# Where the normalised rows and x are transposed inside a slot of the local attention stage

## Chip, cores and metric

The kernel runs on one core of one Trainium2 chip. The metric is the device time of one execution in microseconds (us). The engines are named as in the profile: PE is TensorE (matmul), PEld its weight load, DVE is VectorE, ACT is ScalarE, POOL is GpSimd, SP is SyncE, which here only issues DMAs.

## The reference, cut to what matters

```python
x = x + cross_attention(ctx_1024, layernorm(x), mask)   # 16 heads, 4096 keys
x = x + linear_attention(layernorm(x))                  # two kinds of keys and values
x = x + ffn_stack(layernorm(x))                         # the local stage: 6 layers

# the local stage, x of shape (4, 256, 256), 16 heads of 64, windows of 64
for i in range(6):
    x = attn_layer(shift_tokens(x), Wqkv[i], q_scale[i], k_scale[i], Wo[i]) + x
    x = ffn_layer(shift_tokens(x), ln_g[i], ln_b[i], W1[i], b1[i], W2[i], b2[i]) + x

def attn_layer(x, Wqkv, qs, ksc, Wo):
    q, k, v = split(x @ Wqkv, 3)                  # each (4, 16, 256, 64)
    q, k = rotary(l2norm(q) * qs), rotary(l2norm(k) * ksc)
    # a window of 64 queries looks at its own 64 keys and the 64 before them
    attn = softmax(where(mask, -big, 8 * q @ k.T))
    return (attn @ v) @ Wo

def ffn_layer(x, g, bln, W1, b1, W2, b2):
    a, gate = split((layernorm(x) * g + bln) @ W1 + b1, 2)   # 682 columns each
    return a * gelu(gate) @ W2 + b2
```

`shift_tokens` moves the upper half of the features down by one token.

## The kernel before

The kernel has a stage of cross attention and then one with the linear attention and the six local layers. The change lies in the local layers. One layer is four **slots**, one for each batch of 256 tokens (two tiles of 128). The order of work inside a slot is written out by hand, once for each engine, in a function `slot` of that engine's block; the engines meet only at semaphores, whose counts are given as `a` (the slot's own), `f` (of the slot before) and `n` (of the next). An engine works strictly in the order written.

A slot does three things at a time:

- the **attention** of its own batch: `turn_qk` transposes queries and keys, `scores(g)` makes the scores, DVE's `minima(pair)` (L2334) scales and masks them out of the scores' banks 2 to 5 and counts `s_read`, ACT's `exps(pair)` (L2053) takes the exponent, DVE's `inverse` and `share(pair)` (L2350) normalise, `turn_probs(pair)` (L1772) transposes into bank 6, ACT's `probs_out(pair)` (L2060) copies that to `pT`, `out(g)` (L1788) multiplies with the values, and `project_out` (L1799) with the output weights;
- the **projection** of the next batch: twelve units `project(n, nb, j)` (L1722) into banks 0 and 1 by turns (`DENSE + j % 2`), each copied by ACT's `qkv_out(j)` (L2032) or its like; then on DVE `twists`, `norms`, `cosines`, `sums` (L2300), `scaled_keys` (L2306) turn and scale queries and keys of each tile, with `rotate` on POOL (L2655), a power, between `norms` and `scaled_keys`;
- the **feed-forward** of the batch before: `moments` (L2377) and `normal` (L2393) on DVE, `turn_xn` (L1810) on TensorE, `xn_out` (L2077) on ACT, which makes the high part and the whole of the normalised rows, `xn_low` (L2399) on DVE, which makes the low part; then six pieces `widen(m)` (L1830) into banks 0 and 1, each followed by `gates(m)` (L2097, a Gelu) on ACT and `gated(m)` (L2407) on DVE; then `narrow` (L1841) and `add_ffn` (L2415).

Products are made of parts for precision. A projection unit is six matmuls of 512 columns, of high and low parts. A piece of `widen` takes, for each of its two halves, two matmuls high with high, two high with low, and then two with the low part of the rows; before the first of the latter, and only in `widen(0)`, TensorE waits for `xn_low`:

```python
for n, (px, pw) in enumerate(WIDE_PARTS):
    if m == 0 and px == LOW:
        pe.wait_ge(xnT_done, a + U)
```

`turn_x` (L1705) transposes x of the batch after the next, `x_out` on ACT (L2012, L2013) makes its high part and `x_low` on DVE (L2252, L2253) its low part, for the projections of the slot that follows.

`add_attention` (L2362) adds the attention to x. When it is done, SP sends the half of the features that is to be shifted by one token to the tile `late` (`shift`, L1627 and L1628), and the next slot's `moments` waits for that DMA.

Three kinds of slot have more: batch 0 makes the high parts of the widening weights on ACT (`widening_high`, L2090) and the low parts on POOL (`widening_low`, L2666); batch 2 splits the next layer's projection weights, whose DMAs are issued in the same slot, into high parts on ACT (`weights_high`, L2021) and low parts on DVE (`weights_low`, L2259); batch 3 makes the last of these low parts.

The part of TensorE's slot in question, before the change: unit 9, unit 10, `turn_probs(3)`, unit 11, `turn_xn` (bank 0), `out(1)`, `turn_probs(4)`, `turn_x` (bank 1), `turn_probs(5)`, `widen(0)`, `widen(1)`, `out(2)`, `turn_probs(6)`, `widen(2)`, `turn_probs(7)`, `widen(3)`, `out(3)`, `widen(4)`, `widen(5)`, `project_out`, `narrow`, and then `turn_qk` of the next slot. On ACT: `qkv_out(10)`, `probs_out(3)`, `qkv_out(11)`, `xn_out`, `probs_out(4)`, `x_out`, `exps(7)`, `probs_out(5)`, `gates(0)` (the Gelu needs its table loaded, since `exps` used another), `probs_out(6)`, `gates(1)`. On DVE: `sums`, `share(5)`, `xn_low`, `x_low`, `inverse(7)`, `o_out(1)`, `share(6)`, `gated(0)`.

## Time and profile before

| what | us |
|---|---|
| time, median of 3 runs | 2143.72 |
| lowest and highest | 2138.83 and 2144.59 |
| the profiled execution, its own time | 2145.24 |
| its span, first to last instruction | 2143.4 |
| TensorE busy | 2040.7 |
| VectorE busy | 1723.7 |
| ScalarE busy | 1392.7 |
| GpSimd busy | 550.3 |

The profile covers one execution. The 24 slots of the local stage begin at 781 us. A matmul's end is modelled in the profile, so the time from start to start of two of them is surer than a busy time. "Idle" is the time between the modelled end of an instruction and the start of the next on the same engine.

### The profile page before, as it was taken

The numbers are of one execution on the slowest core, as the hardware profiler recorded it, in microseconds if no ns is written. First come the engines' busy times: TensorE is split into PE (matmuls) and PEld (weight loads), VectorE is DVE, ScalarE is ACT, GpSimd is POOL, SyncE is SP. The second block draws the span as 40 slices with busy tenths as digits, with TensorE's granted clock in tenths as the row PEclk, the third lists the DMA queues.
The fourth block names the chain that finished last, engine by engine and source line by source line (L and its number), as shares of the span: only waits on it lengthen the run. The fifth ranks groups of instructions, "written<-read, shape, count | busy, mean of one in ns | idle before, by whom it ended". The sixth has DMA issues, their size and how long they took to land.

```text
span 2143.4 us, 51804 instructions
## 1 busy us (share of the span) xinstructions
PE 2040.7 (95%) x17400; PEld 1704.1 (80%) x17400; DVE 1723.7 (80%) x4874; ACT 1392.7 (65%) x4026; POOL 550.3 (26%) x317
## 2 busy tenths in 40 slices
PE   5999999999998998999999999999999999999988
PEld 4787887887886676888888888888888888888877
DVE  6786787787676498898889888898889888988883
ACT  3776567567564355676767676866777676767653
POOL 2111111111111334232323233232323242323220
PEclk9999999999999999999999999999999999999999
DMA  3000000000000410021102011201120111011010
GB/s 120 8 10 1 7 12 1 7 12 1 6 26 0 140 31 15 13 72 33 56 14 72 14 58 31 72 14 46 44 73 14 34 57 52 25 33 55 14 33 20
DMA packets 50017, 72.10 MB, mean 34 GB/s; under 512 B 9429, under 2 KB 36869, under 8 KB 49541
## 3 DMA queue, kind: packets, MB, share of 16 engines
q1 hardware_dynamic: 47429, 64.30, 9.9%
q10 hardware_dynamic: 2368, 4.98, 0.6%
q8 instruction: 124, 2.03, 0.4%
q14 instruction: 96, 0.79, 0.1%
HBM read 51.58 MB, written 2.10 MB: 25 GB/s over the span
## 4 chain that ended last, share of the span: by engine, by line
PE 47%; issue 7%; DVE 4%; DMA 3%; ACT 3%; POOL 2%; SPq 1%; DVEq 0%; ACTq 0%; POOLq 0%
PE ps_loc L1722 17%; PE ps_loc L1830 7%; PE ps_loc L1799 5%; PE ps_loc L1761 4%; PE ps_loc L1841 4%; PE ps_loc L1772 4%; DMA late<-y_all 3%; PE ps_loc L1741 3%; PE ps_loc L1788 3%; POOL rnorm L2655 2%; PE ps_loc L1342 1%; ACT xnT_high L2077 1%; ACT pT L2060 1%; ACT xnT_loc L2077 1%; DVE w_low L2259 0%
## 5 line engine op out<-in xcount | busy, mean ns | idle before, releaser
L2655 POOL TENSOR_TENSOR rnorm<-norm_floor,half_loc 128x32 f32<-128x32 f32 x48 | 300.5, 6261 | 582.7 <-DVE norm_floor L2270 385.2
L1722 PE MATMUL ps_loc<-w_high,xT 128*128 128x512 f32 x1152 | 379.3, 410 | 0.7 <-ACT qk L2032 0.6
L2053 ACT ACTIVATE prob_loc<-prob_loc,top_loc 128x128 f32<-128x128 f32 x768 | 299.2, 402 | 45.2 <-DVE top_loc L2334 43.2
L718 ACT ACTIVATE prob<-prob,new_top 128x256 f32<-128x256 f32 x512 | 252.2, 497 | 0.0
L1722 PEld LDWEIGHTS ps_loc<-w_high,xT 128*128 128x128 f32 x1152 | 203.9, 189 | 51.4 <-issue 9.3
L2334 DVE CUSTOM_DVE_ANT_0 prob_loc<-ps_loc,const,rnorm 128x128 f32<-128x128 f32 x768 | 218.8, 345 | 28.0 <-PE ps_loc L1761 25.8
L1722 PE MATMUL ps_loc<-w_low,xT 128*128 128x512 f32 x576 | 228.5, 397 | 0.0
L2045 ACT ACTIVATE qT_loc<-ps_loc 128x512 f32<-128x512 f32 x96 | 57.4, 598 | 238.1 <-PE ps_loc L1741 238.1
L923 DVE CUSTOM_DVE_ANT_0 prob<-ps_cross,bias 128x256 f32<-128x256 f32 x512 | 184.7, 420 | 20.7 <-PE ps_cross L494 11.1
L1799 PE MATMUL ps_loc<-wo,qT_loc 128*128 128x256 f32 x768 | 169.8, 379 | 1.3 <-ACT qT_loc L2067 1.3
L1179 POOL TENSOR_TENSOR o<-o,alpha 128x1024 f32<-128x1024 f32 x32 | 61.0, 1906 | 425.1 <-DVE o L962 333.4
L1799 PEld LDWEIGHTS ps_loc<-wo,qT_loc 128*128 128x128 f32 x768 | 144.1, 190 | 20.1 <-issue 1.4
L2053 ACT ACTIVATION_READ_ACCUMULATOR prob_loc<-prob_loc,top_loc 128x1 f32 x768 | 153.7, 200 | 0.0
L1772 PE MATMUL ps_loc<-const,prob_loc 128*128 128x128 f32 x768 | 123.5, 283 | 30.1 <-ACT pT L2060 21.0
L519 PE MATMUL ps_cross<-const,prob 128*128 128x128 f32 x1024 | 140.4, 280 | 2.8 <-issue 1.9
L2060 ACT ACTIVATE pT<-ps_loc 128x512 f32<-128x512 f32 x192 | 115.1, 600 | 40.3 <-PE ps_loc L1772 28.5
L2350 DVE TENSOR_TENSOR prob_loc<-prob_loc,total_loc 128x512 f32<-128x512 f32 x192 | 132.9, 692 | 3.1 <-DVE total_loc L2343 0.5
L519 PEld LDWEIGHTS ps_cross<-const,prob 128*128 128x128 f32 x1024 | 112.2, 142 | 25.6 <-issue 14.7
L1772 PEld LDWEIGHTS ps_loc<-const,prob_loc 128*128 128x128 f32 x768 | 85.1, 141 | 57.4 <-DVE prob_loc L2350 36.8
L1722 PEld LDWEIGHTS ps_loc<-w_low,xT 128*128 128x128 f32 x576 | 108.3, 188 | 25.7
L1841 PE MATMUL ps_loc<-w,kT_loc 128*128 128x256 f32 x552 | 123.1, 379 | 0.0
L534 PE MATMUL ps_cross<-probT,v 128*64 128x256 f32 x1024 | 121.1, 384 | 0.0
(214 smaller groups left out, 4869.0 us busy)
## 6 DMA issues: line engine op xcount, KB each, us to landing
w_raw<-in_ffn_Wqkv_dram SPq DMA_DIRECT2D x24, 512.0 KB, 5.7
w_raw<-in_ffn_Wqkv_dram SPq DMA_DIRECT2D x24, 256.0 KB, 3.9
wo<-in_ffn_Wo_dram SPq DMA_DIRECT2D x24, 256.0 KB, 3.5
v_mid<-v_even SPq DMA_DIRECT2D x24, 256.0 KB, 3.4
v_mid<-v_odd SPq DMA_DIRECT2D x24, 256.0 KB, 3.7
w<-in_ffn_W_dram SPq DMA_DIRECT2D x12, 341.0 KB, 3.3
w<-in_ffn_W_dram SPq DMA_DIRECT2D x6, 640.0 KB, 4.6
ctx_raw<-in_ctx_dram SPq DMA_DIRECT2D x12, 256.0 KB, 2.8
```

The costliest lines, as they stand in the source:

```text
L519: ins = pe.transpose(ps[:, TURN + t, (i * TT + lt) * P:(i * TT + lt + 1) * P], prob[:, lt, 2 * pair + i, t * P:(t + 1) * P], k.ident)
L718: ins = act.activation(prob[:, t, h, :], prob[:, t, h, :], ACT.Exp, bias=new_top[:, t, h:h + 1], scale=-1.0, accum_out=chunk_sum[:, t, h:h ...
L923: ins = dve.tensor_tensor_reduce(out=prob[:, t, h, :], in0=ps[:, banks[pair % 2] + i, t * CHUNK:(t + 1) * CHUNK], in1=key_bias, scale=1.0, ...
L1722: ins = pe.matmul(ps[:, DENSE + j % 2, :], xT[:, px, kk, t * P:(t + 1) * P], wqkv[pw][:, kk, col:col + 512], start=kk == 0 and n == 0, sto ...
L1772: ins = pe.transpose(ps[:, TURN, at:at + P], prob[:, 2 * (pair % RING) + i, t, :], k.ident)
L1799: ins = pe.matmul(ps[:, WIDE_OUT, t * D:(t + 1) * D], oT[:, pair, t * P:(t + 1) * P], wo[:, pair, :], start=pair == 0, stop=pair == PAIRS - 1)
L1830: ins = pe.matmul(ps[:, DENSE + m % 2, part * T:(part + 1) * T], w1_parts[pw][kk][:, col:col + P], xnT_parts[px][:, kk, :], start=n + kk == 0,
L1841: ins = pe.matmul(ps[:, FFN_OUT, t * D:(t + 1) * D], uT[:, m, t * P:(t + 1) * P], w2[:, m, :], start=m == 0, stop=m == FM - 1)
L2053: ins = act.activation(pr, pr, ACT.Exp, bias=top[:, h, t:t + 1], scale=-1.0, accum_out=total[:, h, t:t + 1])
L2060: act.activation(pT[:, pair % 2, :, :, :].rearrange("p i t q -> p (i t q)"), ps[:, TURN, :], ACT.Copy).then_inc(pT_done, 2)
L2334: ins = dve.tensor_tensor_reduce(out=prob[:, 2 * (pair % RING) + e, t, :], in0=ps[:, bank, cols], in1=band, scale=rnorm[:, b % 2, t, h:h + ...
L2655: pool.tensor_tensor(rnorm[:, b % 2, t, :], norm2_floor[:, :], half[:, :], ALU.pow).then_inc(rnorm_done, 8)
```

## The change

`turn_xn` moves between units 9 and 10 and writes bank 4 (`XN`), one of the scores' banks, which is free once `minima(5)` is done; `xn_out` on ACT moves in front of `qkv_out(11)` and reads that bank. `widen(0)` moves in front of `turn_probs(5)` and waits itself for the copies of the last projection units. `turn_x` moves behind `widen(5)` and writes bank 5 (`XT`); `x_out` moves to the end of ACT's slot and `x_low` on DVE in front of `add_attention`. `turn_qk`, which writes banks 4 and 5 first, waits before its second group for `x_low`. On DVE `xn_low` goes in front of `share(5)`, and `gated(4)` and `gated(5)` go in front of the `cosines` of the second tile. Outside the slots the old bank is kept.

```diff
+        XN, XT = 4, 5
...
-            def turn_x(a, b):
+            def turn_x(a, b, at=None):
 
                 pe.wait_ge(y_out, a + U)
-                pe.wait_ge(qkv_done, a)
+                if at is None:
+                    pe.wait_ge(qkv_done, a)
+                else:
+                    pe.wait_ge(s_read, at + 2 * 6)
+                bank = DENSE + 1 if at is None else XT
...
+                    if g == 1 and turned:
+                        pe.wait_ge(xT_done, a + 2 * U)
...
-            def turn_xn(a, ahead):
+            def turn_xn(a, bank=XN):
                 pe.wait_ge(xn_done, a + U)
-                if ahead:
-                    pe.wait_ge(qkv_done, a + 2 * U + SLOTS - 1)
-                pe.wait_ge(u_done, a)
+                if bank == XN:
+                    pe.wait_ge(s_read, a + U + 2 * 6)
+                else:
+                    pe.wait_ge(u_done, a)
...
                     pe.wait_ge(xnT_copied, a + U)
-                if m == 1 and turn:
-                    pe.wait_ge(xT_done, a + 4 * U)
+                    pe.wait_ge(qkv_done, a + 2 * U + SLOTS - 1 if ahead else a + U)
+                if m == 1 and ahead:
+                    pe.wait_ge(qkv_done, a + 3 * U)
...
                     project(n, nb, 9)
+                if ffn:
+                    turn_xn(f)
+                if ahead:
                     project(n, nb, 10)
                 turn_probs(a, 3)
                 if ahead:
                     project(n, nb, 11)
-                if ffn:
-                    turn_xn(f, ahead)
                 out(a, L, b, 1)
                 turn_probs(a, 4)
-                if turn:
-                    turn_x(L + U * (b + 2), (b + 2) % B)
+                if ffn:
+                    widen(f, fb, 0, ahead)
                 turn_probs(a, 5)
                 if ffn:
-                    widen(f, fb, 0, turn)
-                    widen(f, fb, 1, turn)
+                    widen(f, fb, 1, ahead)
...
-                    widen(f, fb, 4, turn)
-                    widen(f, fb, 5, turn)
+                    widen(f, fb, 4, ahead)
+                    widen(f, fb, 5, ahead)
+                if turn:
+                    turn_x(L + U * (b + 2), (b + 2) % B, a)
                 project_out(a, b)
...
                 probs_out(a, 3)
+                if ffn:
+                    xn_out(f, L if b else L - LAYER, fb)
                 if ahead:
                     qkv_out(n, nb, 11)
-                if ffn:
-                    xn_out(f, L if b else L - LAYER, fb)
                 if split:
                     weights_high(L + LAYER, 0)
                 probs_out(a, 4)
-                if turn:
-                    x_out(L + U * (b + 2))
                 exps(a, 7)
...
                     weights_high(L + LAYER, 11)
+                if turn:
+                    x_out(L + U * (b + 2), XT)
                 if b == 0:
                     widening_high(L, not ffn)
...
                     sums(n, 0)
-                share(a, 5)
                 if ffn:
                     xn_low(f)
+                share(a, 5)
                 if split:
                     weights_low(L + LAYER, 0)
-                if turn:
-                    x_low(L + U * (b + 2))
                 inverse(a, 7)
...
                     norms(n, 1)
-                    cosines(n, 1, 1)
-                    sums(n, 1)
-                    cosines(n, 1, 0)
                 if ffn:
                     gated(f, 4)
                     gated(f, 5)
                 if ahead:
+                    cosines(n, 1, 1)
+                    sums(n, 1)
+                    cosines(n, 1, 0)
                     q_sum(n, 1)
...
+                if turn:
+                    x_low(L + U * (b + 2), XT)
                 add_attention(a, b)
```

## Rows read from the trace of the kernel before

**Rows 1.** The page, busy us (share of the span) and instructions.
```profile
PE 2040.7 (95%) x17400; PEld 1704.1 (80%) x17400; DVE 1723.7 (80%) x4874; ACT 1392.7 (65%) x4026; POOL 550.3 (26%) x317
```

**Rows 2.** Waits of TensorE, 835 to 2069: total us, times, longest.
```profile
PE ps_loc L1772 <- ACT pT L2060: 17.9, 22, 1.7
...
PE ps_loc L1772 <- DVE prob_loc L2350: 2.9, 8, 0.7
PE ps_loc L1830 <- DVE kT_loc L2407: 1.3, 5, 0.3
```

**Rows 3.** Timeline of TensorE, layer 1, batch 1: start, length, count, idle before.
```profile
1087.37 0.60 PE L1772 MATMUL ps_loc<-const,prob_loc 128*128 128x128 f32 x4
1087.72 0.72 PE L1722 MATMUL ps_loc<-w_high,xT 128*128 128x512 f32 x2
...
1091.28 0.60 PE L1705 MATMUL ps_loc<-const,y_all 128*128 128x128 f32 x4
1092.51 0.63 PE L1772 MATMUL ps_loc<-const,prob_loc 128*128 128x128 f32 x4 [0.63 <-ACT pT L2060]
...
1096.96 0.66 PE L1772 MATMUL ps_loc<-const,prob_loc 128*128 128x128 f32 x4
1097.38 0.48 PE L1830 MATMUL ps_loc<-xnT_high,w_high 128*128 128x256 f32 x2
...
1097.93 0.40 PE L1830 MATMUL ps_loc<-xnT_low,w_high 128*128 128x256 f32 x2
...
1104.18 7.07 PE L1799 MATMUL ps_loc<-wo,qT_loc 128*128 128x256 f32 x32
```

**Rows 4.** Timeline of ACT in the same slot.
```profile
1089.95 1.02 ACT L2077 ACTIVATE xnT_high<-ps_loc,vec 128x256 fp32r<-128x256 f32 x2
...
1091.75 0.61 ACT L2060 ACTIVATE pT<-ps_loc 128x512 f32<-128x512 f32 x1
...
1094.30 0.63 ACT L2060 ACTIVATE pT<-ps_loc 128x512 f32<-128x512 f32 x1
1094.94 1.28 ACT L2097 ACT_TABLE_LOAD   x1
1096.23 0.47 ACT L2097 ACTIVATE gate<-ps_loc,vec 128x256 f32<-128x256 f32 x1
1097.74 0.60 ACT L2060 ACTIVATE pT<-ps_loc 128x512 f32<-128x512 f32 x1 [1.03 <-PE ps_loc L1772]
```

**Rows 5.** Timeline of DVE in the same slot.
```profile
1089.33 2.26 DVE L2300 TENSOR_TENSOR qk<-qk,work 128x2048 f32<-128x2048 f32 x1
1091.50 0.68 DVE L2350 TENSOR_TENSOR prob_loc<-prob_loc,total_loc 128x512 f32<-128x512 f32 x1
...
1092.95 0.42 DVE L2252 TENSOR_TENSOR xT<-ps_loc,xT 128x256 fp32r<-128x256 f32 x1 [0.16 <-ACT xT L2013]
...
1096.81 0.48 DVE L2407 SCALAR_TENSOR_TENSOR kT_loc<-ps_loc,vec,gate 128x256 f32<-128x256 f32 x1 [0.89 <-ACT gate L2097]
```

**Rows 6.** Timeline of DVE, layer 1, batch 3.
```profile
1202.40 2.26 DVE L2300 TENSOR_TENSOR qk<-qk,work 128x2048 f32<-128x2048 f32 x1
```

**Rows 7.** Timeline of TensorE, layer 1, batch 3, first matmuls of `project_out`.
```profile
1217.09 1.24 PE L1799 MATMUL ps_loc<-wo,qT_loc 128*128 128x256 f32 x5
```

**Rows 8.** Timeline of ACT, layer 1, batch 2.
```profile
1147.58 0.63 ACT L2021 ACTIVATE w_high<-w_raw 128x512 fp32r<-128x512 f32 x1 [0.40 <-DMA w_raw<-in_ffn_Wqkv_dram]
```

**Rows 9.** Timeline of DVE: layer 1, batch 1, then around the end of layer 2, batch 0.
```profile
1112.52 1.23 DVE L2306 TENSOR_TENSOR qk<-qk,rnorm 128x1024 f32<-128x1024 f32 x1 [1.00 <-issue]
...
1281.10 2.59 DVE L2306 TENSOR_TENSOR qk<-qk,rnorm 128x1024 f32<-128x1024 f32 x1 [1.00 <-issue]
1283.62 0.68 DVE L2362 TENSOR_TENSOR y_all<-ps_loc,y_all 128x512 f32<-128x512 f32 x1
...
1293.15 0.29 DVE L2377 BATCH_NORM_STATS2 stats_loc<-y_all 128x6 f32<-128x128 f32 x1
```

**Rows 10.** Timeline of POOL around the end of layer 2, batch 0.
```profile
1280.98 6.91 POOL L2666 TENSOR_TENSOR w_low<-w,w_high 128x682 fp32r<-128x682 f32 x4
```

More of the change, by code:

```diff
@@ L1724, in project, with turn_qk @@
                 ins.then_inc(qkv_full, 1 if j < SLOTS - 1 else U - SLOTS + 1)
-            def turn_qk(a, first):
+            def turn_qk(a, first, turned):
                 pe.wait_ge(rope_done, a + U)
@@ L1801, in project_out, with widen @@
                 ins.then_inc(y_full, U)
-            def turn_xn(a, ahead):
+            def turn_xn(a, bank=XN):
                 pe.wait_ge(xn_done, a + U)
-                if ahead:
-                    pe.wait_ge(qkv_done, a + 2 * U + SLOTS - 1)
-                pe.wait_ge(u_done, a)
+                if bank == XN:
+                    pe.wait_ge(s_read, a + U + 2 * 6)
+                else:
+                    pe.wait_ge(u_done, a)
                 for kk in range(KD):
                     for t in range(TT):
-                        ins = pe.transpose(ps[:, DENSE, kk * T + t * P:kk * T + (t + 1) * P],
+                        ins = pe.transpose(ps[:, bank, kk * T + t * P:kk * T + (t + 1) * P],
                                            xn[:, t, kk * P:(kk + 1) * P], k.ident)
                 ins.then_inc(xnT_full, U)
-            def widen(a, b, m, turn):
+            def widen(a, b, m, ahead):
                 if m == 0:
@@ L1874, in slot @@
                 n, nb = L + U * (b + 1), (b + 1) % B
-                turn_qk(a, b == 0 and not ffn)
+                turn_qk(a, b == 0 and not ffn, b < B - 1 or turn)
                 scores(a, 0)
@@ L1916, in slot @@
                 if ffn:
-                    widen(f, fb, 2, turn)
+                    widen(f, fb, 2, ahead)
                 turn_probs(a, 7)
                 if ffn:
-                    widen(f, fb, 3, turn)
+                    widen(f, fb, 3, ahead)
                 out(a, L, b, 3)
                 if ffn:
-                    widen(f, fb, 4, turn)
-                    widen(f, fb, 5, turn)
+                    widen(f, fb, 4, ahead)
+                    widen(f, fb, 5, ahead)
+                if turn:
+                    turn_x(L + U * (b + 2), (b + 2) % B, a)
                 project_out(a, b)
@@ L2001, in _ @@
             f = LAYERS * LAYER + U * (B - 1)
-            turn_xn(f, False)
+            turn_xn(f, DENSE)
             for m in range(FM):
@@ L2008, in _, with x_out @@
         def _(act):
-            def x_out(a):
+            def x_out(a, bank=DENSE + 1):
                 act.wait_ge(qkv_full, a)
                 act.wait_ge(xT_full, a + U)
-                act.activation(xT[:, HIGH, 0, :], ps[:, DENSE + 1, 0:T], ACT.Copy)
-                act.activation(xT[:, HIGH, 1, 1:T], ps[:, DENSE + 1, T:2 * T - 1], ACT.Copy).then_inc(xT_high, U)
+                act.activation(xT[:, HIGH, 0, :], ps[:, bank, 0:T], ACT.Copy)
+                act.activation(xT[:, HIGH, 1, 1:T], ps[:, bank, T:2 * T - 1], ACT.Copy).then_inc(xT_high, U)
             def weights_high(L, h):
@@ L2068, in o_out, with xn_out @@
                     .then_inc(o_done, 4)
-            def xn_out(a, L, b):
+            def xn_out(a, L, b, bank=XN):
                 if b == 0:
@@ L2076, in xn_out @@
                     for kk in range(KD):
-                        ins = act.activation(dst[:, kk, :], ps[:, DENSE, kk * T:(kk + 1) * T], ACT.Identity,
+                        ins = act.activation(dst[:, kk, :], ps[:, bank, kk * T:(kk + 1) * T], ACT.Identity,
                                              bias=vec[:, V_FB + kk:V_FB + kk + 1], scale=vec[:, V_FG + kk:V_FG + kk + 1])
@@ L2239, in _ @@
             f = LAYERS * LAYER + U * (B - 1)
-            xn_out(f, LAYERS * LAYER, B - 1)
+            xn_out(f, LAYERS * LAYER, B - 1, DENSE)
             for m in range(FM):
@@ L2248, in by_head, with x_low @@
                 return qk[:, t, :].rearrange("p (s h d) -> p s h d", s=2, d=DH)
[L2250 removed]
+            def x_low(a, bank=DENSE + 1):
                 dve.wait_ge(xT_high, a + U)
[L2252 to L2253 removed]
+                dve.tensor_tensor(xT[:, LOW, 0, :], ps[:, bank, 0:T], xT[:, HIGH, 0, :], ALU.subtract)
+                dve.tensor_tensor(xT[:, LOW, 1, 1:T], ps[:, bank, T:2 * T - 1], xT[:, HIGH, 1, 1:T], ALU.subtract)\
                     .then_inc(xT_done, U)
```

5 lines of the change are left out of this document (1 added, 4 removed).

## Prediction

> **What bounds the kernel now.** I read the page first: TensorE is busy for 95% of the span [rows 1]. So only what TensorE waits for, or does more or less of, can move the time. Next I asked for its waits in the 22 full slots of the local stage, from the second to the last but one [rows 2]. The largest entry is the transpose of probabilities behind ACT's copy to `pT`: 17.9 us in 22 waits, one a slot. The same transpose waits 2.9 us in 8 cases for DVE's shares, and `widen` waits 1.3 us in 5 cases for DVE's gated product. Everything else is under 5 us.
>
> Then I followed one slot, that of batch 1 in layer 1, on three engines in order of time. On TensorE [rows 3] `turn_x` (L1705) starts at 1091.28 and `turn_probs(5)` at 1092.51. Four transposes go 0.35 before the next unit can start (1087.37 to 1087.72), 0.44 before another transpose (an estimate), so the real standstill is 1.23 - 0.44 = 0.8 us; the 0.6 that the view calls idle begins only at the modelled end. On ACT [rows 4] the reason is seen: `xn_out` (L2077) holds the queue from 1089.95 to 1091.75, and only then comes `probs_out(4)`, which `turn_probs(5)` needs. `xn_out` itself was late, because `turn_xn` stood behind the last projection unit. On DVE [rows 5] `sums` (L2300) runs from 1089.33 for 2.26 us, then `share(5)`, `xn_low`, `x_low`. DVE is busy without a break in front of that point, so the end of `sums`, 1091.59, is a fixed date for all that follows it.
>
> **The change on TensorE.** No instruction is added or removed. `turn_xn` moves ahead of unit 10, `widen(0)` ahead of `turn_probs(5)`, `turn_x` from in front of `turn_probs(5)` to behind `widen(5)`. Work is the same but for neighbours (about 0.1 us a slot, dropped). Intended: 1.5 us of `widen(0)` covers the 0.8 us wait.
>
> What `widen(0)` now needs. Its normalised rows: `turn_probs(3)` runs some 0.36 us later than at 1087.37, its copy starts 0.78 behind (the distance 1096.96 to 1097.74 in [rows 3, 4]), takes 0.48, and `xn_out` takes 1.80 plus a tail of 0.13: 1090.9. TensorE comes to `widen(0)` at about 1091.1. In time. But its third pair of matmuls reads the low part, `xnT_low`: in the neighbour `widen(2)` that pair starts 0.55 behind the first (1097.38 to 1097.93), so here at 1091.65. `xn_low` now stands directly behind `sums`: it starts where `share(5)` started, 1091.50, takes 0.68 and ends at 1092.18. TensorE stands still for **0.5 us** inside `widen(0)`, a new wait in the old one's place. Queued behind it are `turn_probs(5)` and everything else of the slot. With 0.95 us of `widen(0)` left, `turn_probs(5)` starts at 1093.2 instead of 1092.51. `share(5)`, now second, ends at 1092.8 and is not late.
>
> **The next wait: the gate.** `widen(2)` waits for `gated(0)`. From `turn_probs(5)` to it there is a chain on ACT and DVE [rows 3 to 5]: copy starts after 0.78, table load after 0.64 more, 1.29 to the Gelu, 0.58 to DVE, 0.48 and 0.05 to TensorE: 3.82 us. TensorE's own work between the two, `widen(1)`, `out(2)` and `turn_probs(6)`, is 3.5 us. So `widen(2)` starts at 1093.18 + 3.82 = 1097.0; before it was 1097.38. That is 0.4 gained, and `turn_x`, paid earlier before, is paid now behind `widen(5)` with 0.42 (1096.96 to 1097.38 is such a turn). From `widen(2)` to `project_out` it is then 6.80 + 0.42 = 7.22: **1104.22 against 1104.18**. In short: `project_out` = end of `sums` + 5.41 + 7.22. Behind `project_out` TensorE runs to the end of the slot without a wait. A plain slot gains nothing: two waits of 0.5 and 0.35 replace one of 0.8.
>
> The table load is ACT's, 1.28 us, and the Gelu follows it at once, 0.01 us later [rows 4]. The Trainium skill, page "ScalarE: Activation LUTs", section "What ACT_TABLE_LOAD costs", counts a further drain of about 1.38 us for a change of set. By the page every `widen(2)` would come 1.4 us later and the kernel some 30 us; the trace disagrees, and the sum uses the trace.
>
> **By kind of slot.** *Batches 0 and 1* (10): +0.04 each, +0.4.
> *Batch 3* (5): `sums` ends at 1202.40 + 2.26 = 1204.66 [rows 6], so `project_out` at 1217.29 where it was 1217.09 [rows 7]: +0.2 each, +1.0.
> *Batch 2* (6): ACT also splits weights there, and `probs_out(4)` stands behind a split that waits for its DMA at 1147.58 [rows 8]. Before the change the chain to `gated(0)` is bound by ACT, and the departure of `x_out` (0.5 us) shortens it. Where the DMA sets the date (two slots) that is 0.5 - 0.42: -0.1 each; where it lands sooner (three) the split moves up too and I take -0.4; the last layer's, without split or `turn_x`, -0.35. Together -1.7.
> *First and last slot*: few or no projections, so TensorE starves and `widen(0)`, or the absence of `x_low`, fills part of a stall. Bounds 0 and 0.8 + 0.7; I take -0.7.
>
> **DVE's tail.** `x_low` goes from the middle to behind `scaled_keys(1)` and costs 0.68 there (an estimate: two instructions of 0.42 [rows 5], each of which overlaps its neighbour by 0.08). `scaled_keys(1)` waits for POOL's power, that for `norms(1)`, and those come 0.67 earlier, since `gated(1)` no longer waits as long: the two cancel, and `add_attention` keeps its date. `gated(4)` and `gated(5)` move behind `norms` and delay only work in front of `scaled_keys(1)`, which waits 1.00 us for POOL anyway [rows 9]. `narrow` did not wait for them, so no gain. `turn_qk`'s new wait for `x_low` is covered: `x_low` ends over 1 us ahead.
>
> `add_attention` matters, for it sends the shifted rows over DMA, and `moments` of the next slot waits for them: ended at 1284.30, used from 1293.15, 8.85 us later [rows 9]. That wait feeds the 2.9 us in [rows 2]. In batch 2 DVE has no slack at its end, so `add_attention` comes 0.2 us later against the slot's end and batch 3 pays: +1.0 in five slots. In batch 0 of the later layers there is a race: `scaled_keys(1)` took 2.59 us, not 1.23 [rows 9, 10], because POOL's `w_low` started at 1280.98, DVE at 1281.10, and both read SBUF. Now the power ends 0.67 earlier and the weights' split, set by `f_full`, 0.4 earlier at most: DVE at 1280.43, POOL at 1280.5 or later. If DVE is first, `add_attention` ends 1.4 us sooner and the waits of batch 1, about three quarters of the 2.9 us plus 0.16 hidden in each of four, go: -2.8. I take it, with 0.6.
>
> The Trainium skill, page "SBUF — State Buffer", section "Who interferes with whom", says that a DVE instruction with two SBUF inputs and a GpSimd one that reads SBUF exclude each other, and that the order of issue decides; by it the loser waits, as the 2.59 us show, and `x_low`, with one input in PSUM, is not touched.
>
> **Sum.** +0.4 + 1.0 - 1.7 - 0.7 + 1.0 - 2.8 = -2.8 us. Against the profiled execution (span 2143.4, time 2145.24) that is 2142.4. The median of the runs is 1.5 lower, 2143.72, which gives 2140.9; I say 2141.
>
> **Rivals.** *A, faster: the wait is really covered.* If `widen(0)` found its low rows in time, `turn_probs(5)` would start behind `share(5)`, 1.3 us earlier at most, and the gate chain would follow: 0.35 a slot, 22 slots, 8 us: 2133. If also the gate came in time, all of [rows 2]'s 17.9 + 1.3, with 0.17 hidden in each of 27, would go: 2143.7 - 24 = 2120. Against: `sums` stands ahead of `xn_low` on DVE in the new order too. Chance 0.2, nearly all for the first half.
> *B, slower: `x_low` at the end delays the shifted rows.* If DVE gains nothing before its tail, `add_attention` is 0.68 late everywhere. It decides where `moments` already waits, 8 slots plus one at the margin: 9 x 0.68 = 6.1, plus batch 3's 1.0: 2150.8. For: DVE's continuous tail in batch 2. Against: POOL's power sets the date in the others. Chance 0.1.
> *C, POOL wins the race.* Then -2.8 falls away: 2143.7, no change that could be told. It and my forecast share 0.7, forecast 0.42, C 0.28.
>
> **Range and chances.** Run to run 0.3% (6.4 us) is what can be told from no change: faster means below 2137.3, slower above 2150.1. Range 2133 (A's first half) to 2149 (most of B). Faster: A plus the low edge of the forecast, 0.25; slower: most of B, 0.08; same 0.67.
>
> **What would show it.** After: `turn_probs(5)` no longer waits for `pT`; instead `widen` waits about 0.3 us (idle; 0.5 real) a slot for `xnT_low`, and 0.1 or more for the gated product, in all slots. Slots of batches 0 and 1 keep their length where nothing else waits. `scaled_keys(1)` at 1.2 us in batch 0 shows the race won, and batch 1's wait for the shifted rows is gone. I am wrong if `widen(2)` starts without a wait (A), or if `moments` waits in most slots (B).

## The result, and the profile after

The kernel with the change takes 2148.54 us (median of 14 runs, 2145.31 to 2152.05); the kernel before, measured beside it, 2144.32 (14 runs, 2138.83 to 2147.91). The ratio is 1.0019, 95% interval 1.0010 to 1.0027: slower by 4.2 us. That is within the 0.3% which the prediction calls the same; but the interval leaves out 1, and a gain of 2.8 us was forecast.

The profiled execution has a span of 2143.9 us (2143.4 before) and a time of 2145.73 (2145.24). In it the part ahead of the local stage, whose code is unchanged, happened to be 2.0 us shorter (the stage begins at 779.1, not 781.1), so the stage itself has grown by 2.5 us, from 1362.3 to 1364.8. The comparison goes by its slots, from the first transpose of one `turn_qk` to that of the next, added up over the layers:

| slots | before | after | difference | forecast |
|---|---|---|---|---|
| batch 0, six | 331.1 | 331.2 | +0.1 | +0.2, less a part of the first slot's 0.7 |
| batch 1, six | 337.4 | 336.1 | -1.3 | +0.2 - 2.8 |
| batch 2, six | 337.8 | 334.9 | -2.9 | -1.7 |
| batch 3, five | 281.7 | 288.4 | **+6.7** | +2.0 |
| the last slot | 74.3 | 74.2 | -0.1 | the rest of the 0.7 |

Nearly everything that grew is in batch 3. The page first (the span, then busy us, share and instructions):

```profile
span 2143.9 us, 51810 instructions
PE 2049.4 (96%) x17400; PEld 1703.0 (79%) x17400; DVE 1720.5 (80%) x4874; ACT 1398.6 (65%) x4026; POOL 529.1 (25%) x317
```

Counts are those of [rows 1]. POOL is 21 us less busy with the same 317 instructions, which will matter below. Waits of TensorE after, 833 to 2070 (total us, times, longest):

```profile
PE ps_loc L1839 <- DVE xnT_low L2410: 7.6, 20, 0.6
PE ps_loc L1779 <- DVE prob_loc L2361: 5.0, 7, 0.9
PE ps_loc L1839 <- DVE kT_loc L2418: 3.4, 5, 1.0
```

Against [rows 2]: the 17.9 us behind `pT` are gone, and `widen` now waits for `xn_low` in nearly every slot, 0.32 idle as a rule (about 0.15 in batch 0 of four layers, 0.59 in batch 3). The entry for DVE's shares has risen from 2.9 to 5.0, and 0.9 is its longest.

**A plain slot went as forecast.** TensorE after, the slot of layer 1, batch 1, which answers to [rows 3]:

```profile
1090.80 0.40 PE L1839 MATMUL ps_loc<-xnT_high,w_low 128*128 128x256 f32 x2
1091.51 0.50 PE L1839 MATMUL ps_loc<-xnT_low,w_high 128*128 128x256 f32 x2 [0.32 <-DVE xnT_low L2410]
...
1092.56 0.60 PE L1779 MATMUL ps_loc<-const,prob_loc 128*128 128x128 f32 x4
...
1096.31 0.51 PE L1839 MATMUL ps_loc<-xnT_high,w_high 128*128 128x256 f32 x2
...
1103.51 0.38 PE L1806 MATMUL ps_loc<-wo,qT_loc 128*128 128x256 f32 x1
```

And DVE there, which answers to [rows 5]:

```profile
1088.59 2.26 DVE L2311 TENSOR_TENSOR qk<-qk,work 128x2048 f32<-128x2048 f32 x1
1090.77 0.68 DVE L2410 TENSOR_TENSOR xnT_low<-xnT_loc,xnT_high 128x512 fp32r<-128x512 f32 x1
1091.37 0.68 DVE L2361 TENSOR_TENSOR prob_loc<-prob_loc,total_loc 128x512 f32<-128x512 f32 x1
```

`sums` ends at 1090.85. By the prediction's formula `project_out` starts 5.41 + 7.22 later, at 1103.48; it starts at 1103.51. From `turn_probs(5)` to `widen(2)` it is 3.75 us (forecast 3.82). The slot is 55.41 long against 55.35. No idle time for the gated product shows in such a slot: the 3.4 us of that entry are the slots of batch 2 but the last, 0.6 to 1.0 each, where the kernel before has 0.26.

**Batch 3.** Layer 1, batch 3. The slot starts at 1173.05 before and at 1171.53 after. The first matmuls of its `turn_probs(0)`, before and then after:

```profile
1183.95 0.66 PE L1772 MATMUL ps_loc<-const,prob_loc 128*128 128x128 f32 x4 [0.15 <-DVE prob_loc L2350]
```

```profile
1183.70 0.66 PE L1779 MATMUL ps_loc<-const,prob_loc 128*128 128x128 f32 x4 [0.93 <-DVE prob_loc L2361]
```

That is 10.90 us into the slot before and 12.17 after: 1.27 of stall, and the slot grew by 1.16. What made the shares late is seen on DVE. Before, from the end of `norms` on (the last line is the first of `moments`):

```profile
1162.83 0.18 DVE L2270 TENSOR_SCALAR norm_floor<-norm 128x32 f32<-128x32 f32 x1
1162.93 1.23 DVE L2294 TENSOR_TENSOR qk<-qk,cos 128x1024 f32<-128x1024 f32 x1
...
1168.46 1.88 DVE L2259 TENSOR_TENSOR w_low<-w_raw,w_high 128x512 fp32r<-128x512 f32 x3
1170.27 1.21 DVE L2306 TENSOR_TENSOR qk<-qk,rnorm 128x1024 f32<-128x1024 f32 x1
1171.40 0.68 DVE L2259 TENSOR_TENSOR w_low<-w_raw,w_high 128x512 fp32r<-128x512 f32 x1
1172.01 0.68 DVE L2362 TENSOR_TENSOR y_all<-ps_loc,y_all 128x512 f32<-128x512 f32 x1
...
1181.40 0.29 DVE L2377 BATCH_NORM_STATS2 stats_loc<-y_all 128x6 f32<-128x128 f32 x1 [0.41 <-DMA late<-y_all]
```

After:

```profile
1160.86 0.18 DVE L2281 TENSOR_SCALAR norm_floor<-norm 128x32 f32<-128x32 f32 x1
1160.95 0.86 DVE L2418 SCALAR_TENSOR_TENSOR kT_loc<-ps_loc,vec,gate 128x256 f32<-128x256 f32 x2
1161.74 1.21 DVE L2305 TENSOR_TENSOR qk<-qk,cos 128x1024 f32<-128x1024 f32 x1
...
1166.66 2.39 DVE L2270 TENSOR_TENSOR w_low<-w_raw,w_high 128x512 fp32r<-128x512 f32 x3
1168.97 1.47 DVE L2317 TENSOR_TENSOR qk<-qk,rnorm 128x1024 f32<-128x1024 f32 x1
1170.36 0.80 DVE L2270 TENSOR_TENSOR w_low<-w_raw,w_high 128x512 fp32r<-128x512 f32 x1
1171.09 0.41 DVE L2263 TENSOR_TENSOR xT<-ps_loc,xT 128x256 fp32r<-128x256 f32 x1
...
1171.75 0.67 DVE L2373 TENSOR_TENSOR y_all<-ps_loc,y_all 128x512 f32<-128x512 f32 x1
...
1181.14 0.29 DVE L2388 BATCH_NORM_STATS2 stats_loc<-y_all 128x6 f32<-128x128 f32 x1 [1.17 <-DMA late<-y_all]
```

`add_attention` ends at 1172.69 before, 0.36 ahead of the slot's start, and at 1172.42 after, 0.89 behind it. The shifted rows are there 8.7 us later in both. The 1.25 us between the two are a sum. `norms` ends 1.30 earlier, counted from the start of batch 2's slot (-1.30). That slot is itself 0.85 shorter on TensorE, so batch 3 starts sooner (+0.85). `x_low` stands in the way (+0.66). Small gaps between dependent instructions come to +0.16. And the low parts and `scaled_keys(1)`, the same five instructions, now take 4.43 us from first start to the end of the group, not 3.55 (+0.88). This last term is nowhere in the prediction. POOL shows where it is from; before:

```profile
1163.15 6.30 POOL L2655 TENSOR_TENSOR rnorm<-norm_floor,half_loc 128x32 f32<-128x32 f32 x1 [19.00 <-issue]
1169.42 2.98 POOL L2643 TENSOR_TENSOR cos<-const,head_scale 128x128 f32<-128x128 f32 x1
```

After:

```profile
1161.18 5.43 POOL L2666 TENSOR_TENSOR rnorm<-norm_floor,half_loc 128x32 f32<-128x32 f32 x1 [17.66 <-issue]
1166.57 0.48 POOL L2654 TENSOR_TENSOR cos<-const,head_scale 128x128 f32<-128x128 f32 x1
1167.02 1.49 POOL L2657 TENSOR_TENSOR sin<-const,head_scale 128x64 f32<-128x64 f32 x2
...
1169.32 2.02 POOL L2657 TENSOR_TENSOR sin<-const,head_scale 128x64 f32<-128x64 f32 x2
```

Before, POOL's power starts at 1163.15, while DVE's first `cosines` is running, which reads two SBUF operands (1162.93 to 1164.16), and it takes 6.30 us. POOL's first table (L2643) then takes 2.98 us beside DVE's low parts, and most of the tables come after `add_attention`'s start. After, the power starts at 1161.18, while `gated(4)` is running, which reads PSUM, and takes 5.43. In both kernels the rest of it runs beside `cosines` and `sums`. What goes with the 0.87 us is therefore the instruction that runs when the power starts. It is so in all eleven traces: the 48 powers of each take 6.28 to 6.30 us where a `twists` or a `cosines` of 1.22 us with two SBUF operands began 0.2 us before them, and 5.42 to 5.43 where it was an instruction that reads PSUM.

After, POOL comes to the tables at 1166.57, just as DVE starts its low parts at 1166.66, and this time it is DVE that loses: three parts 2.39 instead of 1.88, `scaled_keys` 1.47 instead of 1.21, a fourth part 0.80 instead of 0.68. That a power which starts beside a two-operand instruction takes longer fits what the Trainium skill says on the page "SBUF — State Buffer", section "Who interferes with whom" (the second port pair of DVE is GpSimd's only one, and one excludes the other). By that section whoever issues first has the pair for its whole instruction, and here the rows differ: the `cosines` that starts 0.56 us into the power takes 1.21 us, no more than elsewhere. That the loser pays only a part of the other's time, 0.88 us beside 4.8 us of tables, is in the rows alone.

**Batch 1.** The race at the end of batch 0, in layer 2, on DVE and then on POOL, which answers to [rows 9, 10]:

```profile
1279.49 1.23 DVE L2317 TENSOR_TENSOR qk<-qk,rnorm 128x1024 f32<-128x1024 f32 x1
...
1281.30 0.68 DVE L2373 TENSOR_TENSOR y_all<-ps_loc,y_all 128x512 f32<-128x512 f32 x1
```

```profile
1280.36 6.16 POOL L2677 TENSOR_TENSOR w_low<-w,w_high 128x682 fp32r<-128x682 f32 x4 [0.96 <-ACT w_high L2101]
```

DVE starts 0.87 us ahead of POOL, not 0.12 behind it, and the 2.59 are 1.23 again. Counted from the slot's start, the power begins at 44.82 (45.19 before) and `scaled_keys(1)` at 50.33 (51.58). `add_attention` ends 2.64 ahead of batch 1's slot instead of 0.61. `moments` of batch 1 no longer waits in layers 2 to 4; in the last layer the race is still lost, with POOL 0.07 us ahead (`scaled_keys(1)` 2.65).

### The profile page after: what moved, and what is told of

It reads as the page before. It is cut to its first block and busy times, and to the rows that moved or that the text cites. A ratio compares the mean times of both kernels' runs of the same rounds, so it can differ in the third digit from the quotient of the medians.

```text
span 2143.9 us, 51810 instructions
## 1 busy us (share of the span) xinstructions
PE 2049.4 (96%) x17400; PEld 1703.0 (79%) x17400; DVE 1720.5 (80%) x4874; ACT 1398.6 (65%) x4026; POOL 529.1 (25%) x317
## 3 DMA queue, kind: packets, MB, share of 16 engines
HBM read 51.58 MB, written 2.10 MB: 25 GB/s over the span
## 5 line engine op out<-in xcount | busy, mean ns | idle before, releaser
L2666 POOL TENSOR_TENSOR rnorm<-norm_floor,half_loc 128x32 f32<-128x32 f32 x48 | 281.3, 5860 | 572.4 <-DVE norm_floor L2281 381.7
L923 DVE CUSTOM_DVE_ANT_0 prob<-ps_cross,bias 128x256 f32<-128x256 f32 x512 | 184.7, 420 | 20.1 <-PE ps_cross L494 10.6
L1839 PE MATMUL ps_loc<-xnT_high,w_high 128*128 128x256 f32 x528 | 116.5, 302 | 7.1 <-DVE kT_loc L2418 3.4
```

The lines of the kernel that those rows point to most:

```text
L923: ins = dve.tensor_tensor_reduce(out=prob[:, t, h, :], in0=ps[:, banks[pair % 2] + i, t * CHUNK:(t + 1) * CHUNK], in1=key_bias, scale=1.0, ...
L1839: ins = pe.matmul(ps[:, DENSE + m % 2, part * T:(part + 1) * T], w1_parts[pw][kk][:, col:col + P], xnT_parts[px][:, kk, :], start=n + kk == 0,
L2666: pool.tensor_tensor(rnorm[:, b % 2, t, :], norm2_floor[:, :], half[:, :], ALU.pow).then_inc(rnorm_done, 8)
```

## The experiments

Three names stand in the quoted expectations. D: the loss comes from DVE's end, a late `add_attention` and with it late shifted rows in batch 3. W: it comes from TensorE's own new waits in `widen` and from paying `turn_x` behind `widen(5)`. L: what makes DVE's end late is in the main the move of `gated(4)` and `gated(5)`, by way of POOL's earlier tables and DVE's low parts.

Two parts of the profile vary between executions by more than the edits in them explain: the lead-in (778.7 to 783.5 us), whose code is the same in all, and the last slot (73.3 to 77.8). So beside each median stands the length of the 23 slots between. It is 1288.1 us before and 1290.6 after, +2.6.

**The change in three parts.** Each part is made alone on the kernel before. The rows' part: `turn_xn`, `widen(0)`, `xn_out` and `xn_low` moved as in the change; x is turned where it was, into bank 5:

```diff
                 if ffn:
+                    turn_xn(f)
+                if ahead:
                     project(n, nb, 10)
...
                 turn_probs(a, 4)
                 if turn:
-                    turn_x(L + U * (b + 2), (b + 2) % B)
+                    turn_x(L + U * (b + 2), (b + 2) % B, a)
+                if ffn:
+                    widen(f, fb, 0, ahead)
                 turn_probs(a, 5)
```

> Only the rows' part of the change: turn_xn, xn_out, xn_low and widen(0) as in the changed kernel; turn_x, x_out and x_low at their old places (in bank 5); gated(4) and gated(5) behind the cosines again. Theory D (the loss comes from DVE's tail in batch 2, where x_low and the work on POOL make add_attention late, so that moments of batch 3 waits for the shifted rows): the slots of batch 3 stay near 56.4 us as in the kernel before (57.6 in the changed one), the wait of moments there stays at 0.4 us, POOL's power stays at 6.3 us, and the time is that of the kernel before within 3 us, rather below it. Rival W (the new waits inside widen(0) and before widen(2) are the loss): the loss of 2 to 6 us stays.

Measured: 2135.96 us (4 runs), ratio to before 0.9957 (0.9940 to 0.9974); 23 slots 1280.0. Waits of TensorE, 835 to 2061:

```profile
PE ps_loc L1839 <- DVE kT_loc L2418: 5.1, 15, 0.7
...
PE ps_loc L1779 <- DVE prob_loc L2361: 2.2, 7, 0.7
...
PE ps_loc L1839 <- DVE xnT_low L2410: 0.8, 4, 0.3
```

This part is 8.8 us faster. `turn_x` stands between `turn_probs(4)` and `widen(0)` here: the 0.4 us that it takes are covered, because the same time would else be a wait for `xn_low`, which has fallen from 7.6 us to 0.8. The loss did not stay, as W had it. D's marks are there (the power takes 6.3 us, `moments` of batch 3 waits 0.34 to 0.49, its slots take 55.8 to 56.0), but the size was missed: it expected the time of the kernel before within 3 us. Against this part alone the changed kernel's 23 slots are 10.6 us longer: 8.6 of it in batch 3, 2.0 in batches 0 and 1, nothing in batch 2.

The x part: `turn_x` behind `widen(5)`, `x_out` and `x_low` at the ends of their queues, the rest as before:

```diff
-                if turn:
-                    turn_x(L + U * (b + 2), (b + 2) % B)
                 turn_probs(a, 5)
...
                     widen(f, fb, 5, ahead)
+                if turn:
+                    turn_x(L + U * (b + 2), (b + 2) % B, a)
...
+                if turn:
+                    x_low(L + U * (b + 2), XT)
                 add_attention(a, b)
```

> Only the x part: turn_x behind widen(5), x_out at the end of ACT's slot, x_low in front of add_attention; the rows and the gated products as before. turn_probs(5) is released by the same copy at the same time, so turn_x's 0.42 us, hidden in that wait before, is paid in full: 0.4 a slot, 23 slots, 9.7 us. Theory D adds that add_attention comes 0.68 later in every slot and moments waits more where it waited before: 0.6 to 0.7 us in some nine slots, 6 us, so 13 to 16 us slower than before. Rival W: about 10 us slower with the slots of batch 3 longer by 0.4 only.

Measured: 2155.68 us (4 runs), ratio 1.0051 (1.0034 to 1.0068); 23 slots 1296.2. Waits of TensorE, 835 to 2080:

```profile
PE ps_loc L1779 <- ACT pT L2067: 26.1, 22, 1.6
PE ps_loc L1779 <- DVE prob_loc L2357: 6.7, 10, 1.8
```

It is 10.9 us slower. The wait for `pT` is 26.1 us where [rows 2] have 17.9: taking `turn_x` away from in front of it only makes it longer, by 0.37 a slot, and `turn_x` is paid in full elsewhere. Slots of batch 0 grow by 0.4 each. `moments` of batch 3 waits 0.63 to 0.68 instead of 0.34 to 0.52. The time is W's (about 10), not D's 13 to 16: in layer 1 `add_attention` ends 56.4 us into batch 2's slot in both kernels, with `x_low` now in front of it, and against the slot's end it comes 0.2 to 0.3 us later, not 0.7. The slots of batch 3 grow by 0.5 on average.

The third part, `gated(4)` and `gated(5)` alone in front of the `cosines` of tile 1:

```diff
                     norms(n, 1)
-                    cosines(n, 1, 1)
-                    sums(n, 1)
-                    cosines(n, 1, 0)
                 if ffn:
                     gated(f, 4)
                     gated(f, 5)
                 if ahead:
+                    cosines(n, 1, 1)
+                    sums(n, 1)
+                    cosines(n, 1, 0)
```

> The kernel before with one edit on DVE: gated(4) and gated(5) directly behind norms of the second tile, ahead of the cosines. Theory L (POOL's power and a DVE instruction with two inputs in SBUF exclude each other): the power of the second tile takes 5.4 us instead of 6.3, because the instruction beside its start now reads PSUM; scaled_keys is 0.9 us earlier in batches 0, 1 and 3 and the wait of moments in batch 1 goes (2 to 3 us gained); in batch 2 POOL's tables start earlier and run against DVE's low parts and scaled_keys, which lose some 0.9 us, so batch 3 is longer by 0.5 to 0.9 us each (2.5 to 4.5 lost). Net 0 to 2 us slower. Rival: the power's length has nothing to do with its neighbour, it stays at 6.3 and no slot changes by more than 0.1.

Measured: 2148.67 us (10 runs), ratio 1.0016 (1.0006 to 1.0026); 23 slots 1290.1. DVE and then POOL at the end of batch 2, layer 1:

```profile
1170.63 2.39 DVE L2259 TENSOR_TENSOR w_low<-w_raw,w_high 128x512 fp32r<-128x512 f32 x3
1172.94 1.47 DVE L2306 TENSOR_TENSOR qk<-qk,rnorm 128x1024 f32<-128x1024 f32 x1
```

```profile
1165.15 5.43 POOL L2655 TENSOR_TENSOR rnorm<-norm_floor,half_loc 128x32 f32<-128x32 f32 x1 [18.49 <-issue]
```

With no other edit the power is 5.43, the parts 2.39 and `scaled_keys` 1.47, digit for digit as with the whole change. Batch 1 is 2.2 us shorter, batch 2 1.0, and batch 3's five slots are 5.3 longer (1.1 each; at most 0.9 was expected).

In the 23 slots the three parts measure -8.0, +8.1 and +2.0, together +2.1, where the change measures +2.6: they add up within 0.5. The medians add up less closely, to +6.0 against +4.2, with four runs for each of the first two. The change holds a half that wins 0.4% and a half that loses it again.

**The new wait in `widen(0)`.** On the kernel after, DVE's `sums` go behind `share(5)` and `xn_low`:

```diff
-                if ahead:
-                    sums(n, 0)
+                share(a, 5)
                 if ffn:
                     xn_low(f)
-                share(a, 5)
+                if ahead:
+                    sums(n, 0)
```

> The changed kernel with another order on DVE: share(5), xn_low, sums of the first tile, instead of sums, xn_low, share(5). By the chain of the prediction (project_out is the end of sums plus 5.4 plus 7.2) the low rows are then set by ACT's copies, which end 30.0 us into the slot, so xn_low ends at 30.8 instead of 31.26; the wait inside widen(0) (0.33 idle) is gone, turn_probs(5) and widen(2) come 0.3 to 0.4 earlier, in batch 3 0.6. 22 slots: 7 to 9 us faster than the changed kernel, 3 to 6 faster than before. Rival: sums, 2.26 us, now delays inverse(7) and share(6), turn_probs(6) or the gated product waits instead, and nothing or less than 2 us is gained.

Measured: 2140.09 us (10 runs), ratio to before 0.9978 (0.9969 to 0.9988), 8.5 us under the changed kernel; 23 slots 1282.6. DVE and TensorE, layer 1, batch 1:

```profile
1090.37 0.69 DVE L2410 TENSOR_TENSOR xnT_low<-xnT_loc,xnT_high 128x512 fp32r<-128x512 f32 x1 [0.92 <-ACT xnT_loc L2088]
1090.98 2.29 DVE L2311 TENSOR_TENSOR qk<-qk,work 128x2048 f32<-128x2048 f32 x1
```

```profile
1090.85 0.39 PE L1839 MATMUL ps_loc<-xnT_high,w_low 128*128 128x256 f32 x2
1091.12 0.50 PE L1839 MATMUL ps_loc<-xnT_low,w_high 128*128 128x256 f32 x2
```

As expected (7 to 9 us under the changed kernel). The wait for `xn_low` is gone from the list of waits, and a plain slot falls from 55.41 to 54.99. So `sums` was the fixed date that the prediction took it for. `moments` of batch 3 still waits 1.2 us: the two losses are separate.

**The late rows, undone two ways.** On the kernel after, first `gated(4)` and `gated(5)` at their old place in batch 2 only:

```diff
-                if ffn:
+                if ffn and not split:
                     gated(f, 4)
                     gated(f, 5)
                 if ahead:
                     cosines(n, 1, 1)
                     sums(n, 1)
                     cosines(n, 1, 0)
+                if ffn and split:
+                    gated(f, 4)
+                    gated(f, 5)
+                if ahead:
```

> The changed kernel, with gated(4) and gated(5) behind the cosines again in the slots of batch 2 alone. Theory L: there POOL's power takes 6.3 us again, its tables start 0.9 us later and lose against DVE's low parts instead of winning; scaled_keys of that slot takes 1.2 instead of 1.47, add_attention ends 0.7 to 0.9 us earlier, and the slots of batch 3 fall from 57.6 to 56.8 us. The other slots stay. 4 us faster than the changed kernel, that is the kernel before within 2 us. Rival (x_low alone makes batch 3 late): batch 3 stays above 57.4.

Measured: 2143.31 us (10 runs), ratio to before 0.9999 (0.9988 to 1.0009), 5.2 us under the changed kernel; 23 slots 1285.2. POOL, then DVE, at the end of batch 2, layer 1:

```profile
1160.11 6.30 POOL L2670 TENSOR_TENSOR rnorm<-norm_floor,half_loc 128x32 f32<-128x32 f32 x1 [17.65 <-issue]
1166.38 2.98 POOL L2658 TENSOR_TENSOR cos<-const,head_scale 128x128 f32<-128x128 f32 x1
```

```profile
1165.42 1.88 DVE L2270 TENSOR_TENSOR w_low<-w_raw,w_high 128x512 fp32r<-128x512 f32 x3
1167.23 1.21 DVE L2317 TENSOR_TENSOR qk<-qk,rnorm 128x1024 f32<-128x1024 f32 x1
...
1179.02 0.29 DVE L2388 BATCH_NORM_STATS2 stats_loc<-y_all 128x6 f32<-128x128 f32 x1 [0.61 <-DMA late<-y_all]
```

Everything goes back to the numbers of before: 6.30 and 2.98 on POOL, 1.88 and 1.21 on DVE. The wait of `moments` falls from 1.2 to 0.6, and a slot of batch 3 from 57.6 to 56.6. The other slots keep their lengths within 0.15, except batch 1 of the last layer, 0.3 shorter, where DVE won the race this time. `add_attention` ends 0.16 ahead of the slot: 1.05 of the 1.25 us are undone by this edit alone, and the rival of this experiment, `x_low` as the only cause, is out. The 0.20 that are left are the figure of the prediction.

Then, on the kernel after, `x_low` behind `add_attention`:

```diff
+                add_attention(a, b)
                 if turn:
                     x_low(L + U * (b + 2), XT)
-                add_attention(a, b)
```

> The changed kernel with x_low behind add_attention instead of in front of it. Theory D: add_attention of batch 2 ends 0.7 us earlier, moments of batch 3 waits 0.5 instead of 1.2 us, and the slots of batch 3 fall from 57.6 to 57.0, 3 us in all; the price is in turn_qk of batch 3, whose second group now waits for x_low, up to 0.5 us a slot there. Between 1 and 3.5 us faster than the changed kernel. Rival: the copies of keys, not add_attention, set batch 3, and it does not fall.

Measured: 2144.12 us (10 runs), ratio to before 0.9999 (0.9987 to 1.0010), 4.4 us under the changed kernel; 23 slots 1287.5. The wait of `moments` is 0.51 to 0.56, `add_attention` ends 0.23 behind the slot's start (0.66 less), and slots of batch 3 are 0.6 shorter. The price in `turn_qk` came too: it waits 2.3 us in 6 cases for `x_low`. So rival B's price for `x_low` is real, 0.66 us. In the plain slots `add_attention` also ends 0.66 earlier without it (3.24 ahead of the slot, not 2.58), but nothing waits for it there.

**Better versions.** Three kernels were built on the rows' part. The first also has `gated(4)` and `gated(5)` early except in batch 2, and the seventh low part of the weights at the start of batch 3 instead of in front of batch 2's `add_attention`:

```diff
                 if late:
+                    weights_low(L + LAYER, 6)
                     weights_low(L + LAYER, 7)
...
-                if split:
-                    weights_low(L + LAYER, 6)
                 add_attention(a, b)
```

> The rows' part alone, with gated(4) and gated(5) ahead of the cosines in all slots but those of batch 2, and the low part of piece 6 moved from the end of batch 2 to the start of batch 3. Theories D and L: no slot waits for the shifted rows any more (0.3 to 0.8 us before in nine slots), batch 1 takes 55.2 and batch 3 55.7 us; 3 to 4 us faster than the rows' part alone, 11 to 13 faster than before. Rival: moments was no more than a cover for something else (minima, share), and the time is that of the rows' part alone.

Measured: 2138.76 us (12 runs), ratio 0.9969 (0.9958 to 0.9979); 23 slots 1279.5. That is about half of the 11 to 13 us expected against the kernel before. Of the 3 to 4 expected against the rows' part alone there are 0.5 in the 23 slots, and its median is 2.8 higher: the rival's case. Batch 1 is 1.7 us shorter than with the rows' part alone, batch 3 1.8 longer: `moments` of batch 3 no longer waits, but `turn_qk` waits 0.5 for DVE's copies, which now stand behind that low part. The second has, besides, the order of the DVE experiment (`share(5)`, `xn_low`, `sums`, then `x_low`), and batch 2's split of weight piece 1 behind `gates(0)` on ACT and `gated(0)` on DVE:

```diff
                 share(a, 5)
                 if ffn:
                     xn_low(f)
                 if ahead:
                     sums(n, 0)
...
                 if ffn:
                     gated(f, 0)
+                if split:
+                    weights_low(L + LAYER, 1)
```

> The kernel of e7 with two more moves: in batch 2 the high part of piece 1 behind gates(0) on ACT and its low part behind gated(0) on DVE, and on DVE everywhere share(5), xn_low, sums, x_low. Theory G (before widen(2) the chain from turn_probs(5) over ACT's copy, table load and Gelu to DVE is what TensorE waits for): the wait for the gated product in batch 2 falls from 0.7 to about 0.2 us, batch 2 takes 55.4 us, 2 to 4 us faster than e7. Rival: the wait there is for DVE, and nothing changes.

Measured: 2136.34 us (10 runs), ratio 0.9965 (0.9953 to 0.9976); 23 slots 1278.2. Waits of TensorE, 834 to 2058:

```profile
PE ps_loc L1795 <- DVE qT_loc L2367: 9.2, 21, 0.8
PE ps_loc L1748 <- DVE kT_loc L2330: 2.5, 5, 0.5
PE ps_loc L1779 <- DVE prob_loc L2361: 0.5, 3, 0.2
```

Both waits of `widen` are gone, and `out(2)` waits instead, 9.2 us in 21 cases, for `o_out(1)`, which DVE reaches later with `sums` and `x_low` in front of it. Slots of batch 2 take 55.8 us as a rule where 55.4 were expected; against the first version there are 2.4 us by the medians and 1.3 in the 23 slots. The third moves `x_low` behind `o_out(1)` and `share(6)` and puts the seventh low part back where it was:

```diff
                 o_out(a, 1)
                 share(a, 6)
+                if turn:
+                    x_low(L + U * (b + 2), XT)
+                if split:
+                    weights_low(L + LAYER, 0)
```

> The rows' part alone with: gated(4) and gated(5) ahead of the cosines except in batch 2; in batch 2 piece 1's high part behind gates(0) and its low part behind gated(0); DVE's order share(5), xn_low, sums, inverse(7), o_out(1), share(6), then x_low and the low part of piece 0 in the wait for the first gate; the low part of piece 6 back at the end of batch 2. By e8's trace TensorE now waits for DVE's o_out(1) in front of out(2), 0.24 us in most slots and 0.84 in batch 2, because x_low stands ahead of it; with x_low behind share(6) that goes: batches 0 and 1 near 54.9, batch 2 near 55.1, batch 3 near 55.8 us. 3 to 5 us faster than e8's local stage, 12 to 14 us faster than the kernel before. Rival: the gate chain then waits instead and less than 1.5 us is gained on e8.

Measured: 2137.41 us (5 runs; before 2145.68 beside it), ratio 0.9957 (0.9943 to 0.9970); 23 slots 1278.2. Not faster than the one before it, where 3 to 5 us were expected; the rival came. The waits of `out(2)` fall to 2.0 us, those for the gate are back with 5.0, and `moments` of batch 3 waits 0.5 to 0.6 again. These two and the rows' part alone beat the kernel before by 0.4%, and their intervals overlap. The rows' part alone is the simplest of them.

## Why the prediction was wrong

*Plain slots: right.* The new wait in `widen(0)` was forecast at 0.3 idle and is 0.32; the gate chain 3.82 and is 3.75; a slot +0.04 and is +0.06. That `sums` sets the date is shown by the experiment that moves it. The sign set for the gate, a wait of 0.1 or more in all slots, showed in batch 2 and, with 0.11, in one slot of batch 1. The experiments add one thing to the account: the rows' part gains 8.0 us in the 23 slots and the x part, measured on the kernel before, loses 8.1. In a plain slot of the changed kernel the departure of `turn_x` costs some 0.3 us (55.4 against 55.1). In batch 3 `x_low` costs 0.6.

*First and last slot.* -0.7 forecast, -0.3 and -0.1 measured.

*Batch 2: right in sign, but not for the reason given.* -1.7 forecast, -2.9 measured. The gain was put down to the departure of `x_out` from ACT. The rows' part alone, which leaves `x_out` where it was, has the same 334.9 us for these six slots as the whole change; the x part alone, which moves it and pays `turn_x` for it, has 338.0, no less than the 337.8 of before.

*Batch 1: right in sign, too large, and in part by luck.* The power was to end 0.67 us earlier in the slot of the race and DVE to start 50.91 us into it. The power came 0.37 earlier, and DVE started at 50.33 because the power was also 0.87 us shorter, which the prediction did not have. With 6.30 us of power DVE would have come at 51.20 (an estimate from these rows), just when POOL did. With the rows' part alone, where the power is long, DVE lost the race in layers 1, 2 and 5 and won it in 3 and 4. The gain was sized at 2.8 and is 1.3. The prediction took three quarters of the 2.9 us of waits and 0.16 hidden more in each slot. But of the 0.56 to 0.91 by which these slots were longer than a plain one, 0.22 to 0.36 remains with the race won. In layer 2 it is the first `minima`, which starts 5.46 us into the slot and not 5.11, in both kernels; for what it waits was not found. And the race is still lost in the last layer.

*Batch 3: the step that failed.* "In batch 2 DVE has no slack at its end, so `add_attention` comes 0.2 us later against the slot's end and batch 3 pays: +1.0 in five slots." The path is the right one and it is the whole of the loss, but 0.2 measured 1.25 us. What was wrong is the price of `gated(4)` and `gated(5)` in front of the `cosines`. They were costed by their own time on DVE, as "delay only work in front of `scaled_keys(1)`, which waits 1.00 us for POOL anyway". That is read from a row of batch 1. In batch 2 the low parts fill this wait, and POOL, ahead of its old time by the shorter power, runs its tables into them: 0.88 us on DVE, which the sum had at nothing. The third part alone shows these 0.88 us with no other edit, and putting the two instructions back in batch 2 takes 1.05 of the 1.25 away.

The 0.20 that then remain are the forecast's figure, but made up otherwise: `norms` ends 1.30 earlier in the slot and not 0.67, `x_low` costs the 0.66 it was given, and batch 2's own gain on TensorE counts against the hand-over by 0.85, for its slot ends sooner. Over the layers batches 2 and 3 together went from 619.5 to 623.3 us, where +0.3 was forecast.

From the end of `sums` to `project_out` these slots take 0.23 more (forecast 0.2). Both terms make +7.4 in the five slots, and +6.7 was measured: 0.2 to 0.3 us behind `project_out`, which three of them spent before, are gone. There TensorE did not run "to the end of the slot without a wait"; what it waited for was not found.

*The rivals.* A did not come: `xn_low` stood behind `sums`. B's mechanism, `x_low` in front of `add_attention`, came where DVE is full, for 0.66 us in five slots (3.3 of its 6.1). In the plain slots the prediction let the power's earlier date, 0.67, cancel `x_low`. In batch 0 of layer 1 the power starts only 0.37 earlier, and it is again the shorter power that makes `add_attention` end 0.66 sooner. C, POOL winning the race, came in one layer of four.

With the measured terms in place of the forecast ones, +0.1 - 1.3 - 2.9 + 6.7 - 0.1, the stage comes to +2.5, as the trace has it. The medians are 4.2 apart, and the ratio's interval makes that 2.1 to 5.8: it holds the stage's 2.5, so nothing asks for another cause. The profiled execution after is among the four shortest of its 14, and where the other 1.7 us lie no trace shows.

## What to carry to other kernels

When an instruction is moved past others on one engine, look also at who shares a resource with its new neighbours, in every kind of slot: two short reads of PSUM put in front of a run of two-operand SBUF work made another engine's work 0.87 us shorter, which won a race in one kind of slot and lost one in another. Work that stands in front of a wait is free where it stands; `turn_x` cost nothing there. Moving it to a place without a wait costs its full time, even if the wait itself disappears. And where one engine's end has no slack, a gain on another engine in the same slot makes the hand-over later by as much, so the slot that gains and the one that follows have to be summed together. A gain that comes out near its forecast can have another source: only the parts of the change, run one by one, showed that batch 2's was not `x_out`'s.

## What the hardware did that was not expected

- The same POOL power of 128x32 takes 6.28 to 6.30 us or 5.42 to 5.43, and nothing between, in all eleven kernels: of 48 powers 2 are short before, 24 after, and 19 with the two instructions put back in batch 2's five slots. DVE's instruction at the power's start decides which.
- The loser of the contest for SBUF is not always held for the whole of the other's instruction. `scaled_keys(1)` took 1.21 to 1.23 us where it did not lose, 1.47 where it lost to POOL's tables, and 2.57 to 2.71 where it lost to `w_low`. One cosine table on POOL took 0.45 to 0.49, 0.89 to 0.90, 2.38 or 2.98 us.
- The shifted rows were usable 8.7 us after the end of `add_attention` in all three kernels where it was read in layer 1 (before, after, and with the two instructions put back): the wait moves one for one with that end. The 8.85 of [rows 9] are of a slot in which DVE was busy until 0.1 us before.
- The last slot, in which TensorE starves, took 73.3 to 77.8 us over the eleven profiled executions, in step with the TensorE clock granted in it: 73.3 at 0.95, 74.2 to 75.1 at 0.91, 74.7 to 75.4 at 0.89, 76.6 at 0.86, 77.8 at 0.85. The untouched lead-in took 778.7 to 781.1 at 0.99 and 782.5 to 783.5 at 0.98. That is more than the whole effect.
- Whole runs go the same way. Among the 33 runs of the kernel before that stand beside the later experiments, three at 0.986 took 2149.3 to 2150.2 us, eleven at 0.990 took 2143.6 to 2145.0, and the one at 0.994 took 2138.9. A difference of a few microseconds has to be read slot by slot, or between runs of one granted clock.
